# Rounded output projection, sums of squares at the end of TensorE's step, and a floor inside the query/key write, in a two-stage attention kernel

## What is computed

```
x = attn_layer(shift_tokens(x), Wqkv[i], q_scale[i], k_scale[i], Wo[i]) + x
x = ffn_layer(shift_tokens(x), ln_g[i], ln_b[i], W1[i], b1[i], W2[i], b2[i]) + x
```

## Time and profile before

| | us |
|---|---|
| median of 3 runs (4180.85 to 4187.87) | 4187.51 |
| the profiled execution | 4182.92 |
| its span | 4181.1 |
| TensorE busy | 3900.5 (93%) |
| VectorE busy | 3305.5 (79%) |
| ScalarE busy | 3091.6 (74%) |
| GpSimd busy | 2581.2 (62%) |
| TensorE's mean granted clock | 0.986 of full |

### The profile page before, as it was taken

The page is one execution under the profiler, slowest core; times in us unless marked ns, Lnnn a source line. Parts: engine busy times, 40 slices in busy tenths (PEclk is TensorE's granted clock), DMA queues, the critical chain, the costliest instruction groups (busy, mean ns, idle before and its releaser), DMA issues.

```text
span 4181.1 us, 190344 instructions
## 1 busy us (share of the span) xinstructions
PE 3900.5 (93%) x78816; PEld 3039.7 (73%) x78816; DVE 3305.5 (79%) x5294; ACT 3091.6 (74%) x10376; POOL 2581.2 (62%) x2583
## 2 busy tenths in 40 slices
PE   6888885999998999989999989999899999899998
PEld 3555554888866888848888668888488887588884
DVE  6778874988866888938888668989489886698894
ACT  5877785888865888838888658888488886588883
POOL 4667765766645676627666456766377664566660
PEclk9999998999999999999999999999999999999999
DMA  1000001111111111111111111111111111111110
GB/s 35 2 2 2 2 2 53 47 45 45 46 56 38 45 47 45 44 50 44 49 44 46 58 36 47 44 49 42 53 44 47 47 44 61 35 45 46 47 43 26
DMA packets 100195, 167.40 MB, mean 40 GB/s; under 512 B 26224, under 2 KB 33648, under 8 KB 99056
## 3 DMA queue, kind: packets, MB, share of 16 engines
q1 hardware_dynamic: 99312, 154.89, 12.6%
HBM read 26.13 MB, written 2.10 MB: 7 GB/s over the span
## 4 chain that ended last, share of the span: by engine, by line
PE 69%; issue 9%; POOL 3%; DVE 1%; ACT 0%; DMA 0%; SPq 0%; POOLq 0%; DVEq 0%; ACTq 0%
PE s_bank L1177 13%; PE s_bank L1246 10%; PE s_bank L1259 9%; PE s_bank L1198 8%; PE s_bank L1157 5%; PE s_proj L1222 4%; PE s_proj L1223 4%; PE s_proj L1224 4%; PE s_bank L1209 2%; PE s_bank L1210 2%; PE s_bank L1211 2%; PE s_bank L1167 2%; PE s_bank L1140 1%; POOL s_rotated L802 1%; PE s_bank L1289 1%
## 5 line engine op out<-in xcount | busy, mean ns | idle before, releaser
L802 POOL TENSOR_TENSOR s_rotated<-s_rotated,s_by_sin 128x512 f32<-128x512 f32 x768 | 983.8, 1302 | 227.3 <-DVE s_by_sin L1087 225.2
L811 POOL TENSOR_TENSOR s_probs<-s_probs,s_rden 128x256 f32<-128x256 f32 x768 | 479.7, 641 | 729.8 <-DVE s_rden L1027 729.3
L901 ACT ACTIVATE s_probs<-s_bank,s_neg_max 128x64 f32<-128x64 f32 x3072 | 908.0, 310 | 5.7 <-DVE s_neg_max L1020 5.6
L783 DVE TENSOR_TENSOR s_qk<-s_rotated,s_inv_norm 128x1024 f32<-128x1024 f32 x384 | 743.8, 1937 | 11.5
L1082 DVE TENSOR_TENSOR s_rotated<-s_proj,s_cos 128x1024 f32<-128x1024 f32 x384 | 469.6, 1223 | 241.5 <-ACT s_sq L935 240.9
L901 ACT ACTIVATION_READ_ACCUMULATOR s_probs<-s_bank,s_neg_max 128x1 f32 x3072 | 636.1, 207 | 0.0
L891 ACT ACTIVATE s_probs_t<-s_bank 64x512 f32<-64x512 f32 x384 | 226.8, 591 | 524.8 <-PE s_bank L1157 524.8
L1177 PE MATMUL s_bank<-s_qk 32*32 32x64 f32 x49152 | 581.4, 223 | 26.3 <-issue 25.9
L1177 PEld LDWEIGHTS s_bank<-s_qk 32*32 32x32 f32 x49152 | 510.9, 103 | 115.4 <-issue 114.6
L213 POOL TENSOR_TENSOR s_probs<-s_probs,s_rden 128x384 f32<-128x384 f32 (+3 forms) x512 | 406.4, 802 | 206.1 <-DVE s_rden L406 202.2
L824 POOL TENSOR_TENSOR s_sq<-s_sq 128x512 f32<-128x512 f32 x384 | 490.2, 1277 | 65.5 <-ACT s_sq L935 59.8
(11 more groups left out here) (118 smaller groups left out, 8156.2 us busy)
## 6 DMA issues: line engine op xcount, KB each, us to landing
s_v<-s_v SPq DMA_DIRECT2D x384, 192.0 KB, 2.5
s_v<-s_v SPq DMA_DIRECT2D x384, 64.0 KB, 2.4
s_qk<-f_wqk SPq DMA_DIRECT2D x6, 1024.0 KB, 6.4
s_xs_raw<-u SPq DMA_DIRECT2D x48, 128.0 KB
s_xf<-u SPq DMA_DIRECT2D x48, 128.0 KB, 2.3
s_xs_raw<-u SPq DMA_DIRECT2D x48, 127.8 KB
s_xf<-u SPq DMA_DIRECT2D x48, 127.8 KB, 2.6
s_qk<-f_wv SPq DMA_DIRECT2D x6, 512.0 KB, 6.8
```

Of the source, the lines that this page charges most:

```text
L783: return nc.vector.tensor_tensor(qk[:, quad % 2, :, :, at:at + TOKS], rotated[:, par, :, :, :], by, ALU.mult)
L802: nc.gpsimd.tensor_tensor(rotated[:, par, :, half, :], rotated[:, par, :, half, :], by_sin[:, :, 1 - half, :], (ALU.subtract, ALU.add)[half])\
L811: nc.gpsimd.tensor_tensor(part, part, by, ALU.mult).then_inc(S["probs_done"], 1)
L901: last = nc.scalar.activation(probs[:, par, h, b, :], score_bank[h][:, b * KEYS:(b + 1) * KEYS], ACT.Exp, scale=-1.0, bias=neg_max[:, par, ...
```

## The change

The output projection is made of three rounded products (weights and y are split: `y_high` by ScalarE, `y_rest` by VectorE, a new instruction); the projection weights join `w_high` and `w_rest`. TensorE's order in a step becomes: scores, transposes, layer-normalisation product, proj, value-side products (now into `tr_bank`), output projection, value products, sums of squares. The floor instruction on VectorE goes: the logarithm reads the sums from PSUM with a small bias, and the query/key write becomes two instructions that take the minimum with 1e12 and multiply. ScalarE's squares keep their waits; behind them come value copy, logarithm, y, exponential. The layer normalisation's parts run later (its mean one step later, divide and scale at step 0 of the sequence after next), the residual addition at the end of step 4 instead of at the start of step 5.

```diff
 LN_SCALE = 2.0 ** 16
-NORM_FLOOR = 1e-24
+NORM_CUT = 1e12
+LOG_FLOOR = LN_SCALE * 1e-32

+        w_high = sb("s2_w_high", [P, QUADS * 4 * P + INNER + PAIRS * DIM], F32R)
+        w_rest = sb("s2_w_rest", [P, QUADS * 4 * P + INNER + PAIRS * DIM], F32R)
-        wv = [w[:, QUADS * 4 * P:] for w in (w_high, w_rest)]
-        wo = sb("s2_wo", [P, PAIRS, DIM])
+        wv = [w[:, QUADS * 4 * P:QUADS * 4 * P + INNER] for w in (w_high, w_rest)]
+        wo = [w[:, QUADS * 4 * P + INNER:].rearrange("p (a n) -> p a n", a=PAIRS) for w in (w_high, w_rest)]
         probs_t = sb("s2_probs_t", [P, 2, NT, HPG, 2, WIN])
-        y = sb("s2_y", [P, 2, 2, TOKS])
-        w_raw = qk[:, :, :, :, WIN:].rearrange("p a i c t -> p (a i c) t")[:, 0:(QUADS * 4 * P + INNER) // SEQ, :]
+        y_high = sb("s2_y_high", [P, 2, 2, TOKS], F32R)
+        y_rest = sb("s2_y_rest", [P, 2, 2, TOKS], F32R)
+        w_raw = qk[:, :, :, :, WIN:].rearrange("p a i c t -> p (a i c) t")
...
             at = WIN + toks * TOKS
-            by = inv_norm[:, par, :, :].unsqueeze(2).to_broadcast([P, 2, 2, TOKS])
-            return nc.vector.tensor_tensor(qk[:, quad % 2, :, :, at:at + TOKS], rotated[:, par, :, :, :], by, ALU.mult)
+            for i in range(2):
+                by = inv_norm[:, par, i, :].unsqueeze(1).to_broadcast([P, 2, TOKS])
+                last = nc.vector.scalar_tensor_tensor(qk[:, quad % 2, i, :, at:at + TOKS], by, NORM_CUT,
+                                                      rotated[:, par, i, :, :], ALU.min, ALU.mult)
+            return last
...
                 if p == XS_STEP and s < NSEQ - 1:
                     tokens_high(s + 1)
-                if ln and p == LN_STEP + 2:
-                    inverse_std(f)
                 if live(s, p, LAG_VALUE, first):
                     keys_down()
                 if live(s, p, LAG_SCORE, first):
                     exponentials(0)
-                if full:
-                    act.wait_ge(S["v_mm"], n + 1)
-                    nc.scalar.activation(v[:, p // TILES, 2 * (p % TILES), :], vy_bank[:, :], ACT.Copy)\
-                      .then_inc(S["v_done"], 1)
+                if live(s, p, LAG_SCORE, first):
+                    exponentials(1)
                 if ln and p == LN_STEP + 1:
                     centred_square(f)
-                if live(s, p, LAG_SCORE, first):
-                    exponentials(1)
+                if ln and p == LN_STEP + 2:
+                    log_var(f)
                 if full:
                     act.wait_ge(S["proj_done"], n + 1)
                         act.wait_ge(S["ss_done"], n)
                     nc.scalar.activation(sq[:, :, :, :], proj_ps[:, :, :, :], ACT.Square)\
                       .then_inc(S["sq_done"], 1)
+                    act.wait_ge(S["v_mm"], n + 1)
+                    nc.scalar.activation(v[:, p // TILES, 2 * (p % TILES), :], tr_bank[:, :], ACT.Copy)\
+                      .then_inc(S["v_done"], 1)
+                if live(s, p, LAG_MIX, first):
+                    m, par = n - LAG_MIX, place(p, LAG_MIX)[2]
+                    act.wait_ge(S["ss_done"], m + 1)
+                    if not (first and p < LAG_MIX + 2):
+                        act.wait_ge(S["norm_done"], m - 1)
+                    nc.scalar.activation(inv_norm[:, par, :, :].rearrange("p a t -> p (a t)"), ss_bank[:, :], ACT.Ln,
+                                         scale=LN_SCALE, bias=log_floor[:, 0:1]).then_inc(S["log_done"], 1)
                 if live(s, p, LAG_VALUE, first):
                     m = n - LAG_VALUE
                     act.wait_ge(S["pv_done"], m + 1)
                     if not (first and p < LAG_VALUE + 2):
                         act.wait_ge(S["wo_done"], m - 1)
-                    nc.scalar.activation(y[:, place(p, LAG_VALUE)[2], :, :],
-                                         vy_bank[:, :].rearrange("p (a t) -> p a t", a=2), ACT.Copy)\
+                    nc.scalar.activation(y_high[:, place(p, LAG_VALUE)[2], :, :],
+                                         y_bank[:, :].rearrange("p (a t) -> p a t", a=2), ACT.Copy)\
                       .then_inc(S["y_done"], 1)
                 if live(s, p, LAG_MIX, first):
                     m, par = n - LAG_MIX, place(p, LAG_MIX)[2]
-                    act.wait_ge(S["guard_done"], m + 1)
-                    nc.scalar.activation(inv_norm[:, par, :, :], inv_norm[:, par, :, :], ACT.Ln, scale=LN_SCALE)\
-                      .then_inc(S["log_done"], 1)
                     act.wait_ge(S["log_done"], m + 1)
                     nc.scalar.activation(inv_norm[:, par, :, :], inv_norm[:, par, :, :], ACT.Exp, scale=-0.5,
                                          bias=ln_shift[:, 0:1]).then_inc(S["inv_done"], 1)
+                if ln and p == LN_STEP + 2:
+                    inverse_std(f)
...
-                if not first and p == WO_STEP:
...
...
                                           tr_bank[KEYS:P, :].rearrange("p (n q) -> p n q", q=WIN))\
                       .then_inc(S["pt_second"], 1)
+                if live(s, p, LAG_WO, first):
+                    m, par = n - LAG_WO, place(p, LAG_WO)[2]
+                    dve.wait_ge(S["y_done"], m + 1)
+                    nc.vector.tensor_tensor(y_rest[:, par, :, :], y_bank[:, :].rearrange("p (a t) -> p a t", a=2),
+                                            y_high[:, par, :, :].bitcast(F32), ALU.subtract).then_inc(S["y_rest"], 1)
+                if ln and p == LN_STEP + 1:
+                    centre(l * NSEQ + s - 1)
...
-                    dve.wait_ge(S["ss_done"], m + 1)
-                    if not (first and p < LAG_MIX + 2):
-                        dve.wait_ge(S["norm_done"], m - 1)
-                    nc.vector.tensor_scalar(inv_norm[:, par, :, :].rearrange("p a t -> p (a t)"), ss_bank[:, :],
-                                            NORM_FLOOR, None, ALU.max).then_inc(S["guard_done"], 1)
+                if not first and s > 1 and p == 0:
+                    divide(l, s - 2)
+                    scale_shift(l, s - 2)
                 if score:
                     inverse_sum(0)
-                if ln and p == LN_STEP + 2:
-                    divide(l, s - 1)
-                if score:
                     inverse_sum(1)
-                if ln and p == LN_STEP + 2:
-                    scale_shift(l, s - 1)
+                if not first and p == WO_STEP - 1:
+                    r = l * NSEQ + s
+                    dve.wait_ge(S["wo_done"], r * STEPS)
+                    nc.vector.tensor_tensor(seq_of(u_sb, s - 1), wo_bank[:, :], seq_of(u_sb, s - 1), ALU.add)\
+                      .then_inc(S["attn_res"], 1)
...
                         pe.wait_ge(S["pt_second"], m)
+                    pe.wait_ge(S["v_done"], n if s < NSEQ else step_no(l, NSEQ, 0))
                     for e in range(2):
...
                     transposes()
-                if live(s, p, LAG_MIX, first):
...
+                if full and not first and p in (LN_STEP + 1, LN_STEP + 2):
+                    pe.wait_ge(S["log_done"], n - 1)
+                    (ffn_mean if p == LN_STEP + 1 else ffn_var)(l * NSEQ + s - 1)
                 if full:
                     if p == 0:
                         pe.wait_ge(S["xs_rest"], l * NSEQ + s + 1)
-                    if not (first and p < LAG_VALUE + 1):
-                        pe.wait_ge(S["y_done"], n - LAG_VALUE)
...
-                if full:
                     if not (first and p == 0):
                         pe.wait_ge(S["prod_done"], 2 * n)
...
+                if full:
+                    if live(s, p, LAG_VALUE, first):
+                        pe.wait_ge(S["pt_first"], n - LAG_VALUE + 1)
+                        pe.wait_ge(S["pt_second"], n - LAG_VALUE + 1)
+                    if not (first and p == 0):
+                        pe.wait_ge(S["v_done"], n)
...
+                    nc.tensor.matmul(tr_bank[:, :], xs_high[:, s % 2, toks], wv[0][:, cols], start=True, stop=False)
+                    nc.tensor.matmul(tr_bank[:, :], xs_rest[:, s % 2, toks], wv[0][:, cols], start=False, stop=True)\
+                      .then_inc(S["v_mm"], 1)
+                if live(s, p, LAG_WO, first):
+                    m = n - LAG_WO
+                    quad, half, par = place(p, LAG_WO)
+                    pe.wait_ge(S["y_done"], m + 1)
+                    pe.wait_ge(S["y_rest"], m + 1)
+                    if p == LAG_WO and not first:
+                        pe.wait_ge(S["attn_res"], l * NSEQ + s)
+                    for pair in range(2):
+                        into, w = wo_bank[:, half * TOKS:(half + 1) * TOKS], [part[:, 2 * quad + pair, :] for part in wo]
+                        nc.tensor.matmul(into, w[0], y_high[:, par, pair, :], start=(p == LAG_WO and pair == 0),
+                                         stop=False, skip_group_check=True)
+                        nc.tensor.matmul(into, w[0], y_rest[:, par, pair, :], start=False, stop=False, skip_group_check=True)
```

(76 more changed lines are left out.)

29 lines of the change are left out of this document (16 added, 13 removed).

## The result

The changed kernel takes 4647.7 us (median of 4 runs, 4646.4 to 4649.8) against 4187.4 us before: a ratio of 1.111, 95% interval 1.109 to 1.113. The forecast was 4548 us, with 4450 to 4660 as its range.

What follows compares the result with a forecast made beforehand. TensorE's queue bounded the kernel; the change would close a ring of 8.65 us a step against 7.64. +63.6 a layer, -2 and -1, makes +60.6 x 6 + 1 = +365 on 4182.9: 4548 us, range 4450 to 4660.

Steps and rivals of the forecast that it cites:

- the wait of the squares: ScalarE's squares of step n must wait until TensorE's sums of step n-1 have read the one tile sq.
- the ring: Proj, rest of TensorE's step, sums, squares, two VectorE products, proj again: 8.65 us a step against 7.64.
- sums to their release: From the start of TensorE's sums of squares to the start of the waiting engine: 1.07 us.
- releases in the earlier trace take 0.03: A waiting engine starts 0.03 us behind the modelled end of TensorE's group, read from a low-clock case.
- Squares to product: From the start of ScalarE's squares to VectorE's first product: 1.07 us.
- the layers' ends: Tail of each layer, with cheaper projections: 1 us saved a layer.
- The first steps of a layer: Four intervals lacking value products and output projection, partly offset by a lower clock: -2 us a layer.
- Hidden costs: Work the ring covers: layer-norm products (0.86 us), sequencer stalls, and ScalarE, GpSimd and VectorE work under 8.65 us.
- The two writes: VectorE's query/key write as two 512-element instructions: 2.4 us taken, between 1.5 and 4.5, a hidden cost.
- Rival 1: TensorE stays the bound and squares never wait; 0.26 us gained 384 times, 4083 us; chance 5%.
- Rival 2: TensorE, busy about 81%, falls to 1.2 GHz: 13.1 us a step, about 6250 us; chance 3%.
- Rival 3: VectorE becomes the bound through two writes at 4.5 us: 9.2 us a step, 4756 us; chance 7%.

Runs made afterwards that it cites:

- late-sums kernel: The kernel before the change, with only the sums of squares moved behind the output projection at the end of TensorE's step: 4764.0 us, ratio 1.141.
- own tile: The changed kernel, with GpSimd writing the added halves of the squares into a separate tile, so squares wait only for that addition: 4146.1 us, ratio 0.993.
- own tile with fewer waits: The changed kernel with a separate tile for the added squares, minus TensorE waits that another wait in its queue covers: 4117.6 us, ratio 0.987.

## Why the prediction held, and what it mis-sized

**The mechanism** (the wait of the squares, the ring, no engine ahead of it) is shown: the squares idle behind the sums 378 times, opening that one wait gives back all of it, and the output projection taken out of the ring, 0.77 us between the value-side and the value products, shortens a step by 0.75.

**The ring's length** was 8.65 in the forecast and 8.85 in the trace. The term of the sum that was mis-sized is "sums to their release", 1.07 in the forecast and 1.23 measured. Both halves could be read before: a four-record group directly behind the value products lasts 1.13, not 1.03 (the float32 projection in the earlier trace rows, at 1409.31, stood in that place), and at full clock a release by TensorE came 0.10 behind the modelled end, not 0.03 as in the low-clock case of the earlier trace rows: in the earlier trace rows the transposes end at 1412.66, in the earlier trace rows the copy that waits for them starts at 1412.76. The prediction's "releases in the earlier trace rows take 0.03" passed over this row. The late-sums kernel separates them: behind the projection its group lasts 1.03 and the squares start 1.13 after its start. The projection took 0.86 instead of 0.80 with its gap: its first product is 0.18 before the second. Squares to product is 1.05 for 1.07; the other terms agree within 0.02. Together +0.20 x 378 = 76 us of the 100 missed.

**The other 24 us** lie mostly at the layers' ends, where I had saved 1 us each: from the last first-product of a layer to the next layer's first it was 96.2 us on average and is 99.0. The projection waits there for y_rest (24 times, 50.7 us in all), and the mean granted clock of these five stretches is 0.95 where it was 0.97; how much is due to which is not shown. Four layers also have one step of 10.3, some 6 us together. There the granted clock fell to its lower level for a few microseconds (row: us from the span's start, length, busy us and count of PE, PEld, DVE, ACT and POOL, clock, DMA share, GB/s):

```profile
1077.00:1081.00 4.00, 4.00 (x21) 3.71 (x19) 3.41 (x7) 2.41 (x16) 2.68 (x3) 0.57 0.00 1
```

The value-side products last 0.63 us in it instead of 0.39. Before the fall TensorE had been idle 0.33 us ahead of the transposes and 1.24 ahead of proj, in a ring of 9.13; the 1.24 is met in nearly every step without a fall, and two layers have the same 9.1 without one. So what sets it off stays open. The first steps of a layer were right: in the second layer the first four intervals are 32.5 where stiff ones would make 35.4, -2.9 against the -2 forecast.

**Hidden costs.** Layer-norm products cost nothing in the ring, as forecast. The two writes take 1.74 us in the step shown, 2 x 0.87, within the 2.4 assumed; with GpSimd out of the way (own tile) the pair took 1.28, 0.64 for 512 elements:

```profile
1429.78 1.28 DVE L792 SCALAR_TENSOR_TENSOR s_qk<-s_inv_norm,s_rotated 128x512 f32<-128x512 f32 x2
```

The plain products take 1.22 for 1024 elements, 0.61 for 512. So the warning of the Trainium skill, Vector Engine (DVE) Microarchitecture Reference, section "Points that are easy to get wrong", that such an instruction runs at half throughput, does not show in this form of it; the measurement decides. But for the short fall above, the clock stayed at full in the ring. This is the view of the first layer, with the same columns:

```profile
740.00:1200.00 460.00, 407.70 (x9950) 332.45 (x9950) 339.27 (x541) 328.05 (x1166) 271.43 (x268) 1.00 0.14 40
```

TensorE's records cover 407.7 of 460 us, 89%, where I had put 81% of real work.

**Rival 1** (TensorE stays the bound) is refuted for this kernel, and its 4083 us would have been wrong too: with the ring open, and else the same order, the kernel takes 4146. The rounding is worth 0.18 a step and not 0.26, since from its first product to the value products it is 0.79 us and not 0.71, and the late sums cost 0.10 of that (0.97 against 0.87). **Rival 2** (the clock) is refuted as a lasting state; as a fall of a few microseconds it came in 4 of the 378 intervals. **Rival 3** (VectorE) is refuted: VectorE is idle 2.58 us before its first product.

## What to carry to other kernels

When work moves later in one engine's step, look at who still waits for the place where it used to be: a single tile (here `sq`) that was long free becomes the link that closes a ring through three engines, and its length is the sum of all of it. Add the ring up and compare it with the bound engine's step before anything else; if it is longer, give the tile a second copy or split input and output, and check each queue that the moved work now holds up. Take a group's length from one in the same neighbourhood, and release times from a release by the same engine at the same clock.

## What was not expected

In the own-tile kernel, with one more wait in TensorE's queue ahead of the transposes, it is 1.87 us from mask to transposes (median of 378) against 1.72 before, though by the trace that wait's event had long come. With the covered waits left out, when fewer waits stand there than before, the median is 1.81. So only part of it goes with these waits; the cause of the rest stays open. Leaving out covered waits gave 0.6% in all, and the own tile with fewer waits is the fastest of all, 4117.6 us, 1.3% under the kernel before.
